# A two-layer graph network: the next group's first products ahead of the last product, and x2 on VectorE

## The reference

```
h = relu(layernorm(x))
# layer 0: graph attention, 12 heads of 32
hv = h @ W            (12 heads);  th = tanh(hv)
attn = leaky(src(th) + dst(th)^T), masked with -999, softmax over neighbours
f  = elu(attn @ hv + b)
g  = sigmoid(h @ H_w.T + H_b)
x  = x + g * f + (1 - g) * h
# layer 1: masked attention, 6 heads of 64
h = relu(layernorm(x));  q, k, v = h @ Wq + bq, h @ Wk + bk, h @ Wv + bv
x = x + softmax(q k^T / 8 + mask) v @ Wf + bf
```

## Time and profile before

| | |
|---|---|
| median of three runs | 1011.37 us |
| the profiled execution | 1006.25 us |
| its span, first to last instruction | 1004.5 us |
| TensorE busy | 926.7 us (92%) |
| VectorE busy | 786.5 us (78%) |
| ScalarE busy | 641.2 us (64%) |
| GpSimd busy | 278.5 us (28%) |
| mean granted TensorE clock | 0.979 |

### The profile page before, as it was taken

One profiled execution on the slowest core, in us unless ns is written; L12 is line 12 of the kernel. 1 busy time (PEld: TensorE's weight loads), 2 busy tenths in 40 slices (PEclk: granted clock), 3 DMA queues, 4 the chain that ended last, 5 costly groups with the idle time before them and its releaser, 6 DMA issues.

```text
span 1004.5 us, 24765 instructions
## 1 busy us (share of the span) xinstructions
PE 926.7 (92%) x9851; PEld 817.8 (81%) x9851; DVE 786.5 (78%) x1473; ACT 641.2 (64%) x1309; POOL 278.5 (28%) x337
## 2 busy tenths in 40 slices
PE   6599999999999999999999999999999999999595
PEld 5386888988888898888889888888988888898475
DVE  5877777879777787977778797777879777886804
ACT  5647658484865858486585848658584865857242
POOL 2224050331506033150603315060331506032210
PEclk9799999999999999999999999999999999999887
DMA  8303252231526223152522415252241525221102
GB/s 221 66 3 32 34 97 34 71 42 18 97 33 97 33 69 44 19 96 34 97 33 68 45 20 96 33 97 33 69 45 18 96 34 97 33 59 19 20 32 64
DMA packets 185077, 56.41 MB, mean 56 GB/s; under 512 B 166402, under 2 KB 184964, under 8 KB 184964
## 3 DMA queue, kind: packets, MB, share of 16 engines
q1 hardware_dynamic: 184964, 54.83, 31.2%
HBM read 17.07 MB, written 12.58 MB: 30 GB/s over the span
## 4 chain that ended last, share of the span: by engine, by line
PE 71%; DVE 22%; issue 2%; ACT 1%; SPq 1%; DMA 1%; POOL 0%; ACTq 0%; DVEq 0%; POOLq 0%
PE ps L694 12%; PE ps L696 12%; PE ps L695 12%; PE ps L761 8%; PE ps L765 7%; PE ps L762 7%; PE ps L680 5%; DVE p L1072 4%; DVE mx L1070 3%; DVE p L1044 3%; DVE x L1032 3%; PE ps L774 3%; DVE rs L1040 3%; PE ps L897 3%; PE ps L840 1%
## 5 line engine op out<-in xcount | busy, mean ns | idle before, releaser
L439 POOL TENSOR_TENSOR x_in<-x_in,ee 128x384 f32<-128x384 f32 x64 | 68.5, 1070 | 563.9 <-DVE ee L1057 563.9
L426 POOL TENSOR_TENSOR x_in<-x_in,bf_row 128x384 f32<-128x384 f32 x64 | 84.0, 1342 | 50.6 <-ACT p L459 50.6
L1070 DVE TENSOR_REDUCE mx<-ps 128x6 f32<-128x384 f32 x64 | 35.2, 550 | 75.8 <-PE ps L840 75.8
L1085 DVE COPY_PREDICATED_SCALAR z<-not_adj,masked 128x768 f32 x64 | 69.9, 1092 | 29.4 <-ACT z L550 29.4
L955 DVE TENSOR_TENSOR hT1l<-ps,hT1h 128x384 fp32r<-128x384 f32 x128 | 62.5, 549 | 26.0 <-ACT hT1h L464 26.0
L680 PE MATMUL ps<-ident,p 128*128 128x128 f32 x384 | 54.6, 287 | 26.9 <-DVE p L1044 15.5
L680 PEld LDWEIGHTS ps<-ident,p 128*128 128x128 f32 x384 | 44.6, 146 | 32.6 <-issue 18.3
L513 ACT ACTIVATE ps<-hb_all 128x384 f32<-128x384 f32 x56 | 27.6, 493 | 66.9 <-DVE x_in L1097 66.9
L531 ACT ACTIVATE QT<-ps,bq_col 128x512 f32<-128x512 f32 x48 | 33.0, 688 | 58.4 <-PE ps L765 58.4
L694 PE MATMUL ps<-Wf_hi,hT1h 128*128 128x384 f32 x192 | 67.6, 352 | 1.2 <-DVE x L1032 0.6
L432 POOL TENSOR_TENSOR x_in<-x_in,h 128x384 f32<-128x384 f32 x64 | 64.2, 1035 | 14.4 <-DVE Wf_lo L985 14.4
(11 more groups left out here) (134 smaller groups left out, 2815.7 us busy)
## 6 DMA issues: line engine op xcount, KB each, us to landing
x_in<-in_x_dram SPq DMA_DIRECT2D x16, 768.0 KB, 5.0
V<-v_tok SPq DMA_DIRECT2D x64, 192.0 KB, 5.8
V<-v_tok SPq DMA_DIRECT2D x128, 96.0 KB, 2.4
out_dram<-x_in SPq DMA_DIRECT2D x16, 768.0 KB, 3.5
x<-in_L_gnn_H_w_dram SPq DMA_DIRECT2D x1, 576.0 KB, 6.1
QT<-in_L_gnn_W_dram SPq DMA_DIRECT2D x3, 192.0 KB, 6.9
thT<-in_L_gnn_Wq_dram SPq DMA_DIRECT2D x1, 576.0 KB, 5.5
z<-in_L_gnn_Wk_dram SPq DMA_DIRECT2D x1, 576.0 KB, 6.5
```

What stands on the lines that cost most here:

```text
L426: pool.tensor_tensor(x_in[:, j % 3, t], x_in[:, j % 3, t], bf_row[:], ALU.add).then_inc(x2_biased, 1)
L439: pool.tensor_tensor(x_in[:, i % 3, t], x_in[:, i % 3, t], ee[:, t], ALU.subtract).then_inc(x2_made, 1)
L1070: dve.tensor_reduce(mx1[:, q], bank.rearrange("p (h m) -> p h m", m=N), AX_X, ALU.max).then_inc(max1_made, 1)
L1085: dve.copy_predicated(zu, not_adj[:, tiles].unsqueeze(2).broadcast_to((P, 2, PAIRS0, N)), masked0[:].unsqueeze(2).unsqueeze(3).broadcast_t ...
```

## The change

The loop now starts at i = -1, and iteration i also does the first part of layer 0 for group i + 1: its W0 products, tanh, th turned, gate products and srcdst. Iteration -1 does only that for group 0.

TensorE's new order: h1 turned, blocks(0), q(0), blocks(1), q(1), q(2), the Wk projections, the Wv products, all four tiles of the next h turned, the scores, z turned, four attend0, first(0) (the next group's first W0 product), the layer-1 probabilities turned, first(1) to first(3), two attend1, four Wf products, th turned, gate(0), gate(1), srcdst, gate(2), gate(3).

VectorE's close(t) takes over the last step of x2 = x + h - 0.5 (1 + tanh)(h - elu), which GpSimd did, and the row statistics follow in it; GpSimd adds h to x a group earlier. The copies of turned th go from VectorE to ScalarE. ScalarE's pass that made 0.5 + 0.5 tanh goes, since the factor is in close() now. RING follows the new order, and the queues of all engines do too. SP's spread of the layer-0 values comes behind that of layer 1.

```diff
         RING = (
-            jobs("th_made", 0, th_made, 4)
-            + jobs("gate_tanh", 0, gate_tanh, 4)
-            + jobs("thT_copied", 0, thT_copied, 4)
-            + jobs("h1_low", 1, h1_low, 4)
-            + jobs("srcdst_copied", 0, srcdst_copied, 1)
-            + jobs("q_copied", 1, q_copied, 3)[0:2]
+            jobs("h1_low", 1, h1_low, 4)
             + jobs("leaky_made", 0, leaky_made, 8)[0:4]
-            + jobs("q_copied", 1, q_copied, 3)[2:3]
+            + jobs("q_copied", 1, q_copied, 3)[0:1]
             + jobs("leaky_made", 0, leaky_made, 8)[4:8]
+            + jobs("q_copied", 1, q_copied, 3)[1:3]
             + jobs("k_copied", 1, k_copied, 3)
+            + [("spare", None, None, 1, 0)]
             + jobs("values1_made", 1, values1_made, 4)
+            + jobs("h0_low", NEXT, h0_low, 4)
             + jobs("scores1_shifted", 1, scores1_shifted, 4)
             + jobs("probs0T_copied", 0, probs0T_copied, 6)
-            + jobs("attn0_made", 0, attn0_made, 4)[0:3]
-            + jobs("h0_low", NEXT, h0_low, 4)[0:2]
+            + jobs("attn0_made", 0, attn0_made, 4)
+            + jobs("th_made", NEXT, th_made, 4)[0:1]
             + jobs("probs1T_copied", 1, probs1T_copied, 3)
-            + jobs("attn0_made", 0, attn0_made, 4)[3:4]
+            + jobs("th_made", NEXT, th_made, 4)[1:4]
             + jobs("attn1_low", 1, attn1_low, 4)
-            + jobs("h0_low", NEXT, h0_low, 4)[2:4]
             + jobs("out_made", 1, out_made, 4)
+            + jobs("thT_copied", NEXT, thT_copied, 4)[0:3]
+            + jobs("srcdst_copied", NEXT, srcdst_copied, 1)
+            + jobs("gate_tanh", NEXT, gate_tanh, 4)
         )
...
# ScalarE, in order (new)
+                if real(j):
+                    normalise1(j)
+                # tanh of gate(3)
...
+                exp0(3)
+                for t in range(TILES):
+                    copy_values1(t)
                 for q in range(4):
                     put_mask(q)
+                if real(i) and real(i + 1):
+                    h0_parts(i + 1, range(TILES))
...
+                tanh_values(2)
+                tanh_values(3)
+                put_bias(0)
+                put_bias(1)
+                for t in range(TILES):
+                    copy_thT(t)
+                tanh_gate(0)
+                put_bias(2)
+                tanh_gate(1)
+                copy_rows()
+                put_bias(3)
+                tanh_gate(2)
...
# VectorE, close(t)
+                        dve.scalar_tensor_tensor(x1[:, t], h0[:, par, t], 1.0, ee[:, t], ALU.add, ALU.subtract).then_inc(h_less_elu, 1)
+                        dve.wait_ge(h_less_elu, n)
+                        dve.wait_ge(gate_tanh, n)
+                        dve.scalar_tensor_tensor(ee[:, t], gate[:, t], 1.0, x1[:, t], ALU.add, ALU.mult).then_inc(gated, 1)
+                        dve.wait_ge(gated, n)
                         dve.wait_ge(x_plus_h, n)
+                        dve.scalar_tensor_tensor(x_in[:, i % 3, t], ee[:, t], -0.5, x_in[:, i % 3, t], ALU.mult, ALU.add).then_inc(x2_made, 1)
+                        dve.wait_ge(x2_made, n)
                         row_stats(1, x_in[:, i % 3, t], t, i)
...
# VectorE, in order (new)
+                h1 lows; softmax0(0), softmax0(1); norm0(i + 1); softmax0(2), softmax0(3)
+                h0_lows(i + 1, range(TILES))
                 shift1(0), shift1(1), divide1(0), divide1(1), divide0(0) ... divide0(3)
+                close(0), values0(i + 1, 0), values0(i + 1, 1), close(1)
+                attn1 lows, values0(i + 1, 2), values0(i + 1, 3), close(2)
+                add_out(0), close(3), row_sums(1, i), add_out(1), add_out(2)
+                dst_blocks (waits for dst_rows_made and srcdst_full)
+                add_out(3), mask1, not_adj
```

More of the change, by code:

```diff
@@ L286, in last_reader, with bias_by_act @@
                 _, layer, signal, n, k = RING[at]
-                if real(it - layer):
+                if signal is not None and real(it - layer):
                     return signal, (it - layer) * n + (k + 1)
-        def bias_by_act(i):
-            return real(i) and real(i - 2)
+        def bias_by_act(g):
+            return real(g) and real(g - 2)
         def mask_by_act(i):
-            return real(i) and real(i - 1)
+            return real(i - 1)
         def iterations(eng, body):
-            for i in range(groups + 1):
+            for i in range(NEXT, groups + 1):
                 body(i, i % 2)
@@ L346, in body @@
                     load_x(2)
[L347 to L357, removed]
                 if real(j):
@@ L426, in body @@
                         pool.tensor_tensor(x_in[:, j % 3, t], x_in[:, j % 3, t], bf_row[:], ALU.add).then_inc(x2_biased, 1)
[L427 to L430, removed]
+                if real(i + 1):
+                    if real(i):
+                        inv_std(0, i + 1)
+                    pool.wait_ge(h0_made, TILES * (i + 2))
                     for t in range(TILES):
[L432 to L439, removed]
+                        pool.tensor_tensor(x_in[:, (i + 1) % 3, t], x_in[:, (i + 1) % 3, t], h0[:, 1 - par, t], ALU.add)\
+                            .then_inc(x_plus_h, 1)
             iterations(pool, body)
@@ L724, in body, with first @@
                 j = i - 1
-                if real(i):
-                    for t in range(TILES):
+                def first(t):
+                    if real(i + 1):
                         toks = slice(t * P, (t + 1) * P)
-                        pe.wait_ge(h0_low, TILES * i + t + 1)
+                        pe.wait_ge(h0_low, TILES * (i + 1) + t + 1)
                         take(i, job("th_made", t))
-                        if not real(j) and t == TILES - 1:
+                        if not real(i) and t == 2:
                             pe.wait_ge(small_ready, 3)
@@ L742, in body @@
                             take(i, job("gate_tanh", t))
-                            if not real(j) and t == 0:
+                            if not real(i) and t == 0:
                                 pe.wait_ge(small_ready, 5)
@@ L818, in body @@
                     values1(3)
+                if real(i) and real(i + 1):
+                    turn_h0(i, i + 1, 1 - par, range(TILES))
                 def masks():
@@ L1132, in body @@
                     dve.tensor_tensor(bf_row[:], ps[:, job("values1_made", 0) % BANKS, 0:D], bf_row[:], ALU.add).then_inc(bf_made, 1)
+                if real(i) and real(i + 1):
+                    h0_lows(i + 1, range(TILES))
                 shift1(0)
                 shift1(1)
+                divide1(0)
+                divide1(1)
+                divide0(0)
+                divide0(1)
+                divide0(2)
+                divide0(3)
+                close(0)
+                values0(i + 1, 0)
+                values0(i + 1, 1)
+                close(1)
+                if real(j):
+                    for t in range(TILES):
+                        dve.wait_ge(attn1_high, TILES * j + t + 1)
+                        low_tile(hT1l, hT1h, "attn1_low", t).then_inc(attn1_low, 1)
+                values0(i + 1, 2)
+                values0(i + 1, 3)
+                if not real(i):
+                    if real(i + 1):
+                        for n in range(4):
+                            late_lows(n)
+                        source_dest_consts()
+                close(2)
+                add_out(0)
+                close(3)
+                if real(i):
+                    row_sums(1, i)
+                add_out(1)
+                add_out(2)
+                if real(i + 1):
+                    dve.wait_ge(dst_rows_made, i + 2)
+                    dve.wait_ge(srcdst_full, i + 2)
+                    dve.tensor_tensor(thT[:].rearrange("p c m -> p (c m)").rearrange("p (g h m) -> p g h m", g=2, h=HEADS0),
+                                      dst_rows[:].rearrange("p (g m) -> p g m", g=2).unsqueeze(2).broadcast_to((P, 2, HEADS0, N)),
+                                      is_head[:].unsqueeze(1).unsqueeze(3).broadcast_to((P, 2, HEADS0, N)), ALU.mult)\
+                        .then_inc(dst_blocks_made, 1)
+                add_out(3)
                 if real(i):
```

278 lines of the change are left out of this document (116 added, 162 removed).

## The result

The changed kernel takes 1083.89 us (median of 4 runs, 1082.42 to 1084.84), the kernel before 1011.43 in the same comparison: ratio 1.071, 95% interval 1.0685 to 1.0732. It is slower, as forecast, by 72 us where 84 were forecast.

A forecast was written before the change was run, and what follows sets the result against it. It took TensorE to bound the kernel, with small removable waits. 83.5 + 14 x 64.55 + 54.8 + 46.0 = 1088.0 us span; 1.75 outside it gave 1089.8, the 5.1 distance to the median 1095 us; range 1062 to 1120.

The forecast's parts named there:

- 1: end of the Wv products: TensorE from q(0) to the Wv end: 21.16 us before, 20.33 with blocks(0), 0.83, moved ahead of q(0).
- Step 2: ScalarE's masks and first h0 high, then VectorE's four h0 lows, delay shift1 to 4.68 us behind the Wv end, before 0.99.
- Step 3: VectorE runs without a pause from shift1 through softmax, four closes of 2.85 us and row_sums to add_out(1), done at 52.82.
- Step 4: Chain put_bias(1), thT copies, srcdst, dst_blocks, add_out(3), put_bias(3): TensorE waits about 2.1 us; normalise1 follows tanh of gate(2) at 59.89.
- Step 5: From normalise1 to the next q(0), same order as before: 4.66 us, so a group costs 64.55 instead of 58.64.
- The ends: Parts outside the steady groups: 83.5 us ahead of the first mark (+1.8), last interval 54.8 instead of 56.6, last part 46.0.
- The tail: From the last q(0) mark to the end of the span: 46.0 us, +0.8 for masks behind the last value copy.
- with the same distance: Step from profiled execution to median: the kernel before's median lay 5.1 us above its profiled run, assumed again, giving 1095.
- Rival A: The clock falls in every group as TensorE idles some 9 us: half clock 4 us, twice a group; 1116 us, chance 0.10.
- its own counter-argument: Against the falling clock: most of what would be slowed on TensorE lies under ScalarE's and VectorE's parts.
- Rivals B: Faster: VectorE isn't late, add_out(1) ends before TensorE reaches gate(1), the old waits go; 983 or 963 us, chance 0.08.
- C: A draw: only the wait at put_bias(3) is real, early products absorb the rest; 1012 us, chance 0.08.

The follow-up runs named there:

- Experiment 2: Changed kernel with the next h turned after the second Wv product and its parts made beside the last two: 61.47 us per group, ratio 1.0425.
- experiments 3 and 4: Changed kernel with four extra VectorE operations, ahead of close(0) in one, ahead of the h0 lows in the other: 65.98 and 63.73 us per group.
- Experiment 1: Changed kernel with add_out(3) ahead of dst_blocks on VectorE: 62.30 us per group, 1064.26 us, ratio 1.0561.
- experiment 7: Changed kernel with GpSimd's first four x+h adds waiting again for the low parts of the weights: first mark 85.70, time 1081.27 us.
- experiment 3: Changed kernel with four extra VectorE operations of 0.59 us between divide0(3) and close(0): 65.98 us per group, 1126.7 us, ratio 1.1193.
- ninth version: experiment 8 with mask banks re-dealt, values0, attn1 lows, add_out(0), add_out(2), put_bias(3) earlier, normalise1 ahead of the dst rows: 62.85 us per group, ratio 1.0662.
- experiment 5: Changed kernel with x2 back on GpSimd, the factor 0.5 left out, add_out(1) ahead of the last statistics and row sums: 61.46 us per group, ratio 1.0447.
- second version: Changed kernel with the next h turned ahead of all Wv products, each mask right behind its value copy: 61.56 us per group, ratio 1.0427.
- experiment 8: Changed kernel with h turned ahead of Wv products, masks behind value copies, add_out(1) and (3) earlier, GpSimd's first adds waiting again: 59.67 us per group, ratio 1.0153.
- tenth: ninth version with the dst rows back ahead of normalise1 on ScalarE, nothing else changed: 59.72 us per group, ratio 1.0205.

## Why the prediction was right, point by point

The mechanism was right in each step and each was a little too dear, by 0.27, 0.06, 0.07, 0.28 and 0.14 us. Times after the start of q(0), of the group that starts at 406.88:

| step | forecast | measured |
|---|---|---|
| 1: end of the Wv products | 20.33 | 20.06 |
| 2: shift1 starts | 25.01 | 24.68 |
| 3: add_out(1) done, put_bias(1) starts | 52.82 | 52.42 |
| 4: dst_blocks starts | 56.7 | 56.15 |
| 4: normalise1 starts | 59.89 | 59.21 |
| 5: next q(0) | 64.55 | 63.73 |

- Step 2: shift1 starts 4.62 us behind the Wv end (431.56 less 426.94), forecast 4.68, before 0.99. Experiment 2 prices 2.2 of these 3.6 us, at their full length. The rest is covered by TensorE's turning of the next h, 1.47 us long, which stands ahead of the scores in its versions too.
- Step 3: no gap on VectorE from shift1 to add_out(2), and experiments 3 and 4 show that this stretch sets the group. The operation taken as 0.60 measures 0.59 from start to start. The forecast waits of 0.9 at attend1 and 1.3 at Wf measure 0.80 and 1.47. The 2.4 us put on the scores, the turned z and the first attention products measure 1.45 (0.16, 0.40, 0.40 and 0.49); that was too dear, and cost the forecast nothing, since VectorE's stretch set the group.
- Step 4: 6.79 us from put_bias(1) to normalise1 against 7.07; TensorE waits 1.61 for its last bias, forecast 2.1. Experiment 1 shows the wait as a cause: 1.43 a group, where the prediction had about 2.5 come back. What was late next came sooner than it said: the tanh of gate(2) then waits 0.53 us for TensorE.
- Step 5: 4.52 against 4.66.
- The five steps together are 0.82 us a group too dear, 11.5 over fourteen groups. This is the larger part of the miss.
- The ends went the other way: 4.7 us too little ahead of the first mark, where GpSimd's x+h was priced at "Nothing". That held in the steady groups and not in the prologue, since the removed lines also held a wait that kept those adds clear of VectorE's low parts (experiment 7 gives 2.5 to 4.5 of it back). The tail was 2.3 too cheap and the last interval 0.5 too dear. The span is 5.0 us under the forecast: -11.5 and -0.5 against +4.7 and +2.3. So the hit on the whole is in part luck: terms of both signs cancel.
- The other 6 of the 11 us between 1095 and 1083.89 are the step from the profiled execution to the median: it lay 5.1 below the median before, and 1.0 above it now. The rule "with the same distance" had nothing behind it: in four later comparisons the kernel before had medians of 1006.57 to 1008.74, close to the profiled 1006.25.
- Rival A, the clock, had 0.10. It is refuted for this kernel: the windows over the most idle stretches of the group have the granted clock at 1.00. The margin was small: with 2.4 us more idle time in each group (experiment 3) the clock fell in nine groups of fourteen, and there its own counter-argument held: what was slowed lay under VectorE's part in all but one. In the ninth version it fell in every group and did cost time.
```profile
444.00:454.00 10.00, 7.74 (x131) 7.34 (x130) 9.69 (x20) 3.73 (x9) 0.00 (x0) 1.00 0.03 5
462.00:471.00 9.00, 6.79 (x68) 5.16 (x57) 4.27 (x8) 7.03 (x17) 2.34 (x3) 1.00 0.34 99
471.00:476.00 5.00, 5.00 (x35) 3.35 (x34) 4.88 (x6) 3.79 (x9) 1.58 (x2) 1.00 0.45 147
```
- Rivals B and C are refuted: add_out(1) ended when TensorE was at gate(1) (it waited 0.25 us there), and the steps ahead of put_bias(3) were not absorbed.

Where the 5.1 us of a group went: 1.33 come with x2 on VectorE in the old order, 3.8 with the new order on top. The two aren't independent: taken out of the new order, x2 gives 2.27 back (experiment 5, with add_out(1) a little earlier).

## What to carry to other kernels

An in-order queue has a stretch that sets the end and a stretch that waits, and busy shares show neither: the same 2.4 us cost 2.25 in the one and 0.00 in the other. Before work is moved ahead in one engine's order, follow which operations of the others it moves from the idle stretch into the tight one. And a wait in removed lines may have kept two engines apart without anyone having meant it.

## What the runs showed of the hardware

- VectorE operations with two SBUF inputs and GpSimd's hold each other up, in both directions: three W0 low parts 3.10 us instead of 1.50, dst_blocks 2.31 instead of 1.76, and a GpSimd product of 128x4 elements 1.81 instead of 0.20 beside dst_blocks. The mask of the ninth version, with one input of 128x256, took 1.08 beside GpSimd's adds instead of 0.28. By the Trainium skill ("SBUF — State Buffer", SBUF: two separate sides) the two engines share a pair of ports that one of them holds for its whole instruction; the trace agrees, and what is easily overlooked is that the smallest operation pays the whole length of the largest.
- The granted clock stayed 1.00 over a group with 6.38 us idle of 63.73, in pieces of at most 1.6 us. In the ninth version it was 0.82 in 5 us with 1.88 idle, behind 5 us with 1.78 idle. In experiment 3, with a piece of about 3 us in each group, it fell in some groups and not in others that wait as long at the same place (3.01 us in the first group below, 3.16 in the second). The windows below are of two such groups; the sum of the idle time does not tell them apart. From 268 to 274 us the granted clock is 0.50, the lower of its two levels (1.2 GHz), and a matmul of 384 columns takes 0.52 us there instead of 0.34.
```profile
265.00:270.00 5.00, 2.55 (x96) 2.40 (x97) 4.83 (x11) 2.45 (x6) 0.00 (x0) 0.74 0.02 5
270.00:275.00 5.00, 4.97 (x18) 5.00 (x19) 4.86 (x11) 1.21 (x3) 0.00 (x0) 0.58 0.25 32
330.00:335.00 5.00, 1.84 (x58) 1.56 (x58) 4.83 (x10) 0.95 (x2) 0.00 (x0) 1.00 0.00 0
335.00:340.00 5.00, 3.53 (x73) 3.43 (x66) 4.90 (x11) 2.49 (x6) 0.00 (x0) 1.00 0.01 3
```
- By the list of banks, the scores' banks were last written by transposes in two of four score tiles in experiment 2 and in all four in its second version and in experiment 8. Their outputs are off by a relative error of 0.11 and 0.16; those of the ninth and tenth versions, where the scores' banks were last written by Wv products, are not. So the mask that ScalarE had put there seems not to have been added to; which tiles it was follows from the list and was not seen by itself. The Trainium skill ("PSUM — Partial Sum Buffer", PSUM: the matmul accumulator) has each starting matmul clear the written marks of its whole bank, and writes of ScalarE leave the marks alone: three transposes into one bank would leave only the last 128 columns marked, and the scores would overwrite the mask in the others. The runs agree with it and don't show the marks.
